# Splitting the attention weights: four quarters one unit apart instead of four

## The reference

```python
qkv = layernorm(x) @ attn_qkvw + attn_qkvb          # (2, 1024, 3072)
scores = einsum('bhqd,bhkd->bhqk', q, k) * 32 ** -0.5
ctx = einsum('bhqk,bhkd->bhqd', softmax(scores), v)
x = x + ctx @ attn_ow + attn_ob
n = layernorm(x)
out = x + (silu(n @ W_gate.T) * (n @ W_up.T)) @ W_down.T
```

## Time and profile before

| | |
|---|---|
| median of 3 runs | 3275.3 us (3274.19 to 3276.8) |
| profiled execution, its own time | 3276.8 us |
| its span, first to last instruction | 3275.2 us |
| granted TensorE clock, mean | 0.988 |
| PE busy | 3172.7 us, 97% |
| DVE busy | 2000.2 us, 61% |
| ACT busy | 1451.6 us, 44% |
| POOL busy | 802.4 us, 24% |
| all 96 `wl` on DVE | 83.0 us, 871 ns each |
| all 96 `wh` on POOL | 79.4 us, 831 ns each |

### The profile page before, as it was taken

One profiled execution on the slowest core, in us unless ns is written; L12 is line 12 of the kernel. 1 busy time (PEld: TensorE's weight loads), 2 busy tenths in 40 slices (PEclk: granted clock), 3 DMA queues, 4 the chain that ended last, 5 costly groups with the idle time before them and its releaser, 6 DMA issues.

```text
span 3275.2 us, 38853 instructions
## 1 busy us (share of the span) xinstructions
PE 3172.7 (97%) x14464; PEld 2485.3 (76%) x14464; DVE 2000.2 (61%) x3098; ACT 1451.6 (44%) x2679; POOL 802.4 (24%) x599
## 2 busy tenths in 40 slices
PE   6999999999999999998899999999999999999999
PEld 5767777766777677766677888888888888888887
DVE  5788888888898898988873332323233433233324
ACT  1478777877787787876670111111111111111111
POOL 1224333333344343434332101010101010101010
PEclk8999999999999999998999999999999999999999
DMA  2434333442343424335438511111111411111111
GB/s 104 126 104 130 98 117 92 133 146 78 106 118 98 143 83 121 99 120 176 118 110 260 187 51 53 52 39 48 56 65 55 177 51 46 39 58 48 49 52 52
DMA packets 146029, 315.90 MB, mean 96 GB/s; under 512 B 24945, under 2 KB 58865, under 8 KB 142257
## 3 DMA queue, kind: packets, MB, share of 16 engines
q1 hardware_dynamic: 145840, 313.42, 30.8%
HBM read 228.41 MB, written 84.41 MB: 96 GB/s over the span
## 4 chain that ended last, share of the span: by engine, by line
PE 86%; DVE 9%; ACT 1%; DMA 1%; issue 1%; SPq 1%; POOL 0%; DVEq 0%; ACTq 0%
PE ps L650 16%; PE ps L651 16%; PE ps L652 16%; PE ps L716 6%; PE ps L735 6%; PE ps L747 6%; PE ps L752 6%; PE ps L805 5%; PE ps L806 5%; PE ps L807 5%; DVE mx L1037 3%; DVE pl L1059 3%; DVE wl L1009 1%; PE ps L677 1%; SPq L1183 1%
## 5 line engine op out<-in xcount | busy, mean ns | idle before, releaser
L874 ACT ACTIVATE pu<-ps 128x512 f32<-128x512 f32 x1024 | 616.3, 602 | 362.5 <-PE ps L735 359.0
L1037 DVE TENSOR_REDUCE mx<-ps 128x1 f32<-128x512 f32 x1024 | 696.6, 684 | 128.4 <-PE ps L716 118.2
L1137 POOL TENSOR_TENSOR pl<-pu,ph 128x512 fp32r<-128x512 f32 x315 | 425.8, 1352 | 950.4 <-ACT ph L875 949.7
L875 ACT ACTIVATE ph<-ps 128x512 fp32r<-128x512 f32 x1024 | 613.8, 599 | 0.0
L1059 DVE TENSOR_TENSOR pl<-pu,ph 128x512 fp32r<-128x512 f32 x709 | 552.4, 780 | 58.2 <-ACT ph L875 55.1
L650 PE MATMUL ps<-x2h,gh 128*128 128x512 f32 x1376 | 535.4, 389 | 0.8 <-DVE x2l L1003 0.8
L651 PE MATMUL ps<-x2h,gl 128*128 128x512 f32 x1376 | 535.3, 389 | 0.0
L652 PE MATMUL ps<-x2l,gh 128*128 128x512 f32 x1376 | 535.3, 389 | 0.0
L1099 DVE TENSOR_TENSOR hf<-ps,sg 128x512 f32<-128x512 f32 (+1 forms) x88 | 60.9, 692 | 693.9 <-PE ps L652 685.3
L716 PE MATMUL ps<-kst,qst 96*128 96x512 f32 x1024 | 417.7, 408 | 20.8 <-DVE mx L1037 17.6
L735 PE MATMUL ps<-qst,kst 98*128 98x512 f32 x1024 | 411.2, 402 | 5.1 <-ACT ph L875 3.9
(11 more groups left out here) (91 smaller groups left out, 4529.8 us busy)
## 6 DMA issues: line engine op xcount, KB each, us to landing
wraw<-in_wqkv SPq DMA_DIRECT2D x24, 1024.0 KB, 5.7
qst<-q_d SPq DMA_DIRECT2D x192, 128.0 KB, 3.0
kst<-k_d SPq DMA_DIRECT2D x192, 128.0 KB, 3.1
graw<-in_wg SPq DMA_DIRECT2D x44, 512.0 KB, 4.6
graw<-in_wu SPq DMA_DIRECT2D x42, 512.0 KB, 3.5
draw<-in_wd SPq DMA_DIRECT2D x42, 512.0 KB, 4.1
q_d<-stg SPq DMA_DIRECT2D x64, 256.0 KB, 2.4
k_d<-stg SPq DMA_DIRECT2D x64, 256.0 KB, 2.3
```

Of the source, the lines that this page charges most:

```text
L874: e.activation(pu[sl][:, :], bk[:, :], ACT.Exp, scale=SCALE).then_inc(s["a_p"], 1)
L875: e.activation(ph[sl][:, :], bk[:, :], ACT.Exp, scale=SCALE).then_inc(s["a_ph"], 1)
L1037: e.reduce_max(mx[:, j % 2, t, half:half + 1], ps[2 + bank_of["a", j, t, half]][:, :], AX.X).then_inc(s["v_mx"], 1)
```

## The change

The quarters of the splits of all 24 loads are deferred one unit apart. For loads 3 to 23 the second, third and fourth `whi` move 3, 6 and 9 units ahead, and the `wlo`s with them; loads 0 to 2 stay as they are.

```diff
             step("wload", n)
             for q in range(4):
-                defer(5 + (4 if n > 2 else 1) * q, "whi", n, q)
+                defer(5 + q, "whi", n, q)
             loads[0] += 1
```

## The result

The kernel with the change takes 3306.7 us (median of 6 runs, 3301.3 to 3308.4), the one before 3276.9 in the same session: a ratio of 1.0087, 95% interval 1.0075 to 1.0099. By the ratio it is 28.5 us slower (29.8 by the medians), and the forecast of 3278 with a range to 3294 missed it. The profiled execution after took 3301.7 us, 25 more than that of before, so the traces show a little less than the medians.

A forecast was written before the change was run, and what follows sets the result against it. PE sets the time in the attention loop, DVE close behind. Gains 2.7, 1.2, 1.2 and 7 against losses 13.6, 0 (batch turn) and 1.5 give + 3.0 us: from 3275.3 to 3278 us, range 3265 to 3294.

The forecast's parts named there:

- the clusters: Four `wl` in a row on DVE, loads 5 to 11 and 14 to 23: 0.8 us lost each, 13.6 together, bounds 3.4 and 27.
- load 17: POOL's `cdiv` and `pl` delay the later `wh`, so DVE waits: 1.5 us lost on PE, bounds 0 and 3.
- (c): First product of load 14: PE's 1.08 us wait for the last `wlo` at 838.65 goes, gain 1.2 us.
- (a): Load 3, values of group 1: PE's 2.68 us wait and low clock at 118 us go, net gain 2.7 us.
- (b): Load 4 issued some 6 us earlier, its splits leaving the loop's first units: gain 1.2 us, bounds 0 and 3.
- (d): `wl`s leave loop units where DVE was late, giving back part of PE's 11.7 us waits: gain 7, bounds 3 and 10.
- a reserve of 1.3: In the attention loop, how many us late `mx` may be before `a` waits; 1.8 at most, 0.7 as lower bound.
- The two examples: Places in the trace before: around 402 us 2.3 us extra work without waits; around 1118 to 1123 3.0, some 0.5 lost.
- Every cluster stalls `a` for more than a microsecond: Rival: DVE falls behind at each of 17 places, 1.5 us each, + 15 us, 3290 us; chance 0.21.
- The clock rival: Stalls also lower PE's granted clock, half of the 17 places costing 1.6 us more: + 28, 3303 us; chance 0.11.
- A `pl` of POOL that holds a context product: Sign of being wrong: `pl` on POOL so late that a context product waits; costed at nothing.

The follow-up runs named there:

- The high parts alone: Against the kernel before: loads 3 to 23 with `whi` on POOL one unit apart, `wlo` on DVE still four apart; 3279.3 against 3277.4 us, ratio 1.0006.
- the low parts alone: Against the kernel before: loads 3 to 23 with `whi` still four units apart, `wlo` one apart behind the last `whi`; 3302.2 us, ratio 1.0079.
- the low parts on POOL: Against the kernel before: all `wlo` moved from DVE to POOL, quarters still four units apart; 3261.6 against 3276.5 us, ratio 0.9956.
- the low parts six units later: Against the changed kernel: for loads 3 to 23 each `wlo` six units behind its `whi` instead of two; 3303.3 us, ratio 1.0083 to the kernel before.
- two units apart: Against the kernel before: quarters of loads 3 to 23 two units apart instead of four; 3291.4 against 3276.5 us, ratio 1.0043.

## Why the prediction was wrong

**The bound** was read rightly: PE sets the time, DVE's `mx` is what holds it, and POOL and the DMAs play no part. The high parts alone and the low parts alone show that. One reading in it was wrong, and nothing hangs on it: the attention loop doesn't end about 1560 us. Its last `p` starts at 1714.7 in the trace of before and the first matmul of `gate_up` at 1847.7, so the window from 1640 us still holds the last part of the loop.

**The sum** was + 3.0 us and the traces show + 25.0. Of the 22.0 between them the clusters are 14.3 (29.4 against 13.6 and the 1.5 for load 17), the relief with (c) 5.0 (3.2 against 8.2), and the start, (a) and (b), 2.7 (1.2 against 3.9).

**(a) Load 3.** Right in kind, forecast 2.7 us net. Timeline of SP, DVE and PE after:

```profile
112.58 0.68 DVE L1009 TENSOR_TENSOR wl<-wraw,wh 128x512 fp32r<-128x512 f32 x1
...
114.58 0.50 PE L716 MATMUL ps<-kst,qst 96*128 96x512 f32 x1 [0.66 <-DVE mx L1037]
...
114.79 0.45 SPq L1183 DMA_DIRECT2D wraw<-in_wqkv  x1
```

The fourth `wl` is at 112.58 instead of 117.61, the gap of 2.68 us is gone and with it the low clock behind it (granted clock 1.00 from 113 to 123 us, 0.64 before). The cluster's price is the 0.66 us at 114.58. Unit 0 begins 1.9 us earlier, not 2.7.

**(b) Load 4.** Wrong: the gap of 1.03 us before `mx` is still there at 128.62, and the first 20 units take 0.7 us more, not 1.2 less. The load was issued at 114.8, 3.8 us earlier in place of the 6 I gave it, and with the loop beginning earlier too, its first `wl` still stands in the loop's first units, and the other three now come with it.

**(c) Load 14.** Right: no wait for `wl` is left in the loop.

**(d) Relief of the other units**, 7 us with bounds 3 and 10: too much. Outside the clusters' stretches PE's waits for `mx`, `mm` and `ml` fell by only 1.3 us, from 9.5 to 8.2, and the time by 3.2 with (c) in it. The wrong thought was that waits near a `wl` are waits by a `wl`. With the low parts on POOL the waits for `mx` didn't fall either (8.8 us against 8.5), but that isn't a test of DVE without them, since its `pl`s were longer there.

**The clusters**: the step that failed most, 0.8 us for each of 17, 13.6 together with an upper bound of 27; measured 1.7 each, 29.4. Mechanism, direction and place were as said. At load 8 the room was as I had it: three units of 1.46 and a reserve of 1.3 make 5.7 us, and PE wanted the third `mx` 5.7 us behind the first `wl`. What I missed is the work in it. First, `pl` was costed at 0.60 us throughout, and only `wl` at a higher price beside POOL, 1.1 us, which is its price beside a `wh`. A late DVE meets POOL's own `pl` with its `wl` or `pl`, and that costs up to 1.8 (last section): over the 17 clusters the `wl`, `pl` and `cl` beyond 0.70 us, in the stretch that DVE works without a pause, add up to 2.1 us each, where I had 1.2 for the `wl`s. Mean `pl` rose from 767 to 791 ns, 13.8 us over 574 of them, while `wl` rose from 871 to only 882, less than the 900 to 1000 that I expected:

```profile
L1059 DVE TENSOR_TENSOR pl<-pu,ph 128x512 fp32r<-128x512 f32 x574 | 453.8, 791 | 44.5 <-ACT ph L875 41.6
L1009 DVE TENSOR_TENSOR wl<-wraw,wh 128x512 fp32r<-128x512 f32 x72 | 63.5, 882 | 0.0
```

Second, the other work (`stg`, `cl`, `vt`, `mm` and its copies) was taken at 0.3 us. Between the first and the fourth `wl` that holds, 0.24 us on the mean; but DVE is late for longer than four units, and up to its next pause it is 1.05. Load 19 shows both. Timeline of DVE and PE, kernel after:

```profile
1163.64 1.43 DVE L1009 TENSOR_TENSOR wl<-wraw,wh 128x512 fp32r<-128x512 f32 x1
1164.99 1.75 DVE L1059 TENSOR_TENSOR pl<-pu,ph 128x512 fp32r<-128x512 f32 x1
...
1167.39 0.79 PE L716 MATMUL ps<-kst,qst 96*128 96x512 f32 x1 [2.29 <-DVE mx L1037]
1167.98 0.63 PE L747 MATMUL ps<-ph,vt 128*65 128x512 f32 x1
```

A `vt` and an `mm` fall in the cluster, `wl` and `pl` are long, PE stands 1.45 us for `mm` and 2.29 for `mx`, and the matmuls behind are slow: 5.7 us. Once the room is used up, what comes on top is lost nearly one to one, as at load 8. So the loss at a place isn't that of the mean place, and a sum made from a mean cluster can't give it. The two examples couldn't show it. Around 402 us the second `wl` starts 6.2 us behind the first, just outside the four units of 5.84, so the work in them was about 1.7 us and not 2.3, less than the 1.8 that a mean stretch has free. Around 1118 us there is one `wl`. Neither tested a crowd.

How much each of the two contributes isn't settled. In the run with the low parts six units later the lengthening is less (1.3 us a cluster) and the loss is the same; PE's idle time grew by 16.0 us there and not 20.9, and the lower clock level makes up the difference (table below). Nor is it settled why the changed kernel's first seven clusters got off so lightly: from unit 20 to 439 it loses 2.6 us, and the other two placements of the clusters 11.5 and 7.1. In the second batch every placement loses, 17 to 24 us from unit 439 to unit 900.

**Load 17**: POOL was not late for `wl`; the waits of `wl` for `wh` are the same two as before, ahead of the loop. Its cluster cost 3.0 us, like others with a `cl` and an `stg`.

**The rivals.** "Every cluster stalls `a` for more than a microsecond", 3290 us, was the right one, and it passed its own point of 1.2 us. Its number was built on the same gains of 12 us, of which 4.4 came. The clock rival, which has the nearest number, isn't what happened in the changed kernel, but it is not nothing either. The mean granted clock is 0.988 as before; from 1148 to 1230 us, with load 19 in it, it is 0.98 where it was 1.00. From unit 20 to unit 900 the traces have, in us:

| | time | PE idle | at the lower level |
|---|---|---|---|
| before | 1343.2 | 32.9 | 10.2 |
| the change | 1369.4 | 53.8 | 13.7 |
| low parts alone | 1371.6 | 50.5 | 27.3 |
| low parts six behind | 1369.6 | 48.9 | 23.9 |
| two units apart | 1362.0 | 43.9 | 23.9 |

At the lower level a matmul takes 0.79 or 0.80 us in place of 0.40, so as an estimate the clock costs half of the extra time there: 1.7 us of the change's 26.2, and 7 to 9 of the other three's 28.4, 26.4 and 18.8. Why it fell so much more often there isn't shown. What is left of the 26.2, beside 20.9 of idle time and 1.7 of clock, is what a stall costs beyond its idle time: 0.27 us at load 8 (1.89 lost, 1.62 idle), which makes 4.9 us for 18 more waits for `mx` and `mm`, an estimate. A `pl` of POOL that holds a context product, costed at nothing, cost nothing here, and 8.5 us where POOL had the low parts too.

## What to carry to other kernels

Here an engine that is not the bound but works 90% of the time had room for one extra operation in several units, not for four in a row. Look at the first deadline behind the crowd: count every operation of the engine up to it, at the duration it has when it runs late and beside its neighbours, not at its best. And before crediting relief to work that is moved away, count the waits place by place: of the 7 us credited here, 1.3 us of waits went. What was worth having lay elsewhere: the low parts on POOL, 15 us faster, 9 of them from the first five loads.

## What the runs showed of the hardware

That POOL slows DVE's two-input operations was in the first trace (1.1 us in place of 0.68), and so was a `wl` of 1.75. Timeline of POOL there, kernel before:

```profile
1119.56 1.29 POOL L1137 TENSOR_TENSOR pl<-pu,ph 128x512 fp32r<-128x512 f32 x1 [2.84 <-ACT ph L875]
```

The price isn't a fixed one: it depends on which of the two began first. In the trace after, 92 times a `wl` or `pl` of DVE starts while one instruction of POOL is running and no other follows within it. Each ends 0.53 to 0.56 us behind the end of POOL's, however much of that was left; the `wl` above ends 0.55 behind (1121.40 and 1120.85). In 46 cases DVE began first, and its operation kept its 0.67 to 0.69 us; POOL's own `pl` then took up to 1.82 us, where 1.28 to 1.30 is usual alone. So the row at 400.80 is long, 1.77 us, because POOL's `pl` had begun at 400.26, and that one is long, 1.76, having begun just behind DVE's `wl` of 400.20. `mx`, which reads PSUM, stays at 0.69 us or less beside either. Beside a `wh` alone, a `wl` or `pl` took 1.13 us at most, about the 1.1 that the forecast used; beside a `pl` of POOL alone up to 1.79.
